# Two early mean subtractions moved behind later gates in the finish of a four-layer triangle-update kernel

## The reference

```
for each layer:
    xn    = layernorm(groupnorm(x))
    left  = (xn @ Wl [+ bl]) * sigmoid(xn @ Wlg [+ blg])     # two layers with a mask
    right = (xn @ Wr [+ br]) * sigmoid(xn @ Wrg [+ brg])
    out   = contraction of left and right over one token index, per channel
    x     = x + gated, projected layernorm(out)
```

## Time and profile before

| | |
|---|---|
| median of 3 runs | 2207.23 us (2206.90 to 2209.74) |
| the profiled execution's own time | 2204.45 us |
| its span (first to last instruction) | 2202.4 us |
| mean granted TensorE clock | 0.965 of full speed |
| TensorE busy | 1970.2 us (89%) |
| VectorE busy | 1734.3 us (79%) |
| ScalarE busy | 1655.7 us (75%) |
| GpSimd busy | 624.5 us (28%) |

### The profile page before, as it was taken

How to read it: one execution, slowest core, us unless ns; L and a number is a source line. 1 busy time by engine, 2 the same in 40 slices (tenths; PEclk the granted TensorE clock), 3 DMA queues, 4 the chain that set the end, 5 groups by cost and what they waited for, 6 DMA issues and landing times. The chain is left out here.

```text
span 2202.4 us, 45933 instructions
## 1 busy us (share of the span) xinstructions
PE 1970.2 (89%) x13950; PEld 1401.2 (64%) x13956; DVE 1734.3 (79%) x2934; ACT 1655.7 (75%) x2442; POOL 624.5 (28%) x590
## 2 busy tenths in 40 slices
PE   5798979699898998989989899899998989899998
PEld 4433959455433988965633598886553369798665
DVE  6788989989588878878958897877775888687664
ACT  3588869679788857758978785766877887596676
POOL 0100818265200000026410280732871000000655
PEclk8999999999999999989999999999999999999999
DMA  9488938279698928259979973917997984663798
GB/s 397 164 266 285 290 77 229 92 286 384 231 279 264 309 77 296 87 214 396 416 224 279 273 191 129 286 45 262 406 391 221 281 303 157 223 200 125 285 358 303
DMA packets 429363, 549.48 MB, mean 249 GB/s; under 512 B 14640, under 2 KB 325936, under 8 KB 412848
## 3 DMA queue, kind: packets, MB, share of 16 engines
q1 hardware_dynamic: 427648, 538.38, 73.1%
q10 hardware_dynamic: 1584, 9.51, 1.1%
HBM read 371.67 MB, written 176.16 MB: 249 GB/s over the span
## 5 line engine op out<-in xcount | busy, mean ns | idle before, releaser
L799 PE MATMUL bank<-whigh,kept 128*128 128x128 f16 x4096 | 507.5, 227 | 60.0 <-DMA kept<-XH 23.6
L799 PEld LDWEIGHTS bank<-whigh,kept 128*128 128x128 f16 x4096 | 466.9, 125 | 67.4 <-issue 53.9
L799 PE MATMUL bank<-wlow,kept 128*128 128x128 f16 x4096 | 506.5, 227 | 0.0
L799 PEld LDWEIGHTS bank<-wlow,kept 128*128 128x128 f16 x4096 | 467.5, 125 | 0.0
L1558 POOL TENSOR_TENSOR LR<-LR 128x512 f32<-128x512 f32 x128 | 186.6, 1477 | 526.6 <-DVE LR L1604 509.6
L821 ACT ACTIVATE sigs<-bank,small 128x256 f32<-128x256 f32 x512 | 237.2, 476 | 60.3 <-PE bank L799 53.6
L1549 POOL TENSOR_TENSOR LR<-LR,sum 128x2048 f32<-128x2048 f32 x30 | 136.6, 4552 | 510.2 <-DVE LR L1366 510.2
L663 PE MATMUL bank<-LR,cen 128*128 128x512 f32 x512 | 254.4, 622 | 21.3 <-DMA LR<-XT 9.5
L821 ACT ACTIVATE squares<-bank,small 128x256 f32<-128x256 f32 x512 | 236.2, 476 | 13.8 <-PE bank L799 6.6
L670 PE MATMUL bank<-LR,kst 128*128 128x512 f32 x512 | 240.9, 593 | 5.2 <-ACT LR L691 5.2
L836 POOL TENSOR_TENSOR msgs<-sigs,mask_sb 128x256 f32<-128x256 f32 x192 | 126.1, 672 | 378.6 <-ACT sigs L821 373.6
(11 more groups left out here) (174 smaller groups left out, 3616.4 us busy)
## 6 DMA issues: line engine op xcount, KB each, us to landing
kept<-XH SPq DMA_DIRECT2D x128, 512.0 KB, 6.0
LR<-XT SPq DMA_DIRECT2D x64, 1024.0 KB, 9.5
kept<-XHA SPq DMA_DIRECT2D x128, 512.0 KB, 4.6
LR<-XT SPq DMA_DIRECT2D x112, 512.0 KB, 5.4
XT<-LR SPq DMA_DIRECT2D x56, 1024.0 KB, 8.5
LR<-XH SPq DMA_DIRECT2D x64, 512.0 KB, 6.6
LR<-XHA SPq DMA_DIRECT2D x64, 512.0 KB, 5.7
OS<-kept SPq DMA_DIRECT2D x12, 2048.0 KB, 7.6
```

The lines of the kernel that those rows point to most:

```text
L799: last = pe.matmul(bank(g)[:, j * P:(j + 1) * P], tokens, w[:, half * P:(half + 1) * P], start=part == 0, stop=part == 1)
```

## The change

The subtraction of chunk 2 moves from step 7 to step 9 (`GL + 2`), that of chunk 3 from step 11 to step 12 (`GL + 5`), in the layers with the gate first. All other chunks stay.

```diff
             def _(dve):
                 def normalize(t):
-                    c = (t + AHEAD) // 4
-                    if (t + AHEAD) % 4 or not 0 < c < NCH:
+                    later = {2: GL + 2, 3: GL + 5} if gate_first else {}
+                    c = next((c for c, at_tile in later.items() if at_tile == t), (t + AHEAD) // 4)
+                    if later.get(c, 4 * c - AHEAD) != t or not 0 < c < NCH:
                         return
                     if c >= len(nrm):
                         dve.wait_ge(turned.s, turned.n + 4 * (c - len(nrm)) + 4)
```

## The result

| | before | after |
|---|---|---|
| median of 16 runs each | 2205.53 us (2201.33 to 2211.28) | 2210.7 us (2207.14 to 2216.01) |
| ratio of the times, 95% interval | | 1.0025 [1.0016, 1.0033] |
| the profiled execution's own time, and its span | 2204.45, 2202.4 us | 2209.22, 2207.3 us |
| mean granted TensorE clock | 0.965 | 0.958 |

The account below looks back on a forecast made before the run. TensorE was taken to set the pace in a finish's second half, its front pauses hanging on VectorE and GpSimd. +1.21 + 0 + 0 = +1.2 us took 2207.23 to 2208.4 us, range 2205.3 to 2211.3.

Parts of the forecast that it names:

- price of one fall: One tile behind the pause at half clock, 4.27 us for 1.94, 2.3 us lost: 2210.7 us in all, chance 0.07.
- The wait at s(2): VectorE's 2.83 us stand before chunk 2's subtractions, s(2), first finish: becomes other work, while the subtraction starts 1.65 us later.
- a(0): VectorE's residual add of tile 0, behind which chunk 2's subtractions were to stand in the first finish.
- p(1): TensorE's output product of tile 1: its pause, 1.05 us in the first finish and 0.60 in the second, was to go.
- The link of 7.10: From one chunk's subtractions to the next over GpSimd's multiply, 7.10 us: chunk 3's come +1.65 us, chunk 4's +1.21, first finish.
- p(17): TensorE's output product of tile 17, after a 2.07 us pause in the first finish: forecast 1.21 us later, at 486.07.
- The second finish: Finish of the second layer: depends on when TensorE's clock rises, taken as 0, with -0.7 to +1.0 us kept.
- Behind the third place: After chunk 6's subtractions wait 2.50 us for GpSimd's multiply of chunk 5: TensorE has no idle time to absorb anything.
- The chain's sum: Both finishes together: +1.21 for the first, 0 for the second, 0 for the moments' length, +1.2 us.
- The moments' own length: GpSimd's second-half moments, between its multiplies of chunks 4 and 5: taken as 0, with -0.5 us kept for each finish.
- The clock falls at the third place: Rival: pause before tile 17's output product grows to about 2.6 us; one fall 2210.7 us (0.07), two 2214.0 (0.04).
- a 0.50 clock behind p(17): Sign that the forecast is wrong: granted TensorE clock at 0.50 after tile 17's output product.

Follow-up runs that it names:

- before_fill: The kernel before, with tile 20's three out-gate matmuls issued four times over in both gate-first finishes: median 2209.01 us, ratio 1.0014.
- before_shift: The kernel before, with nine small extra matmuls behind each of the two gate-first finishes: median 2208.55 us, ratio 1.0021.
- before_again: The kernel before, unchanged, timed once more as a program of its own: median 2207.83 us, ratio 1.0002.
- after_again: The changed kernel, unaltered, timed a second time as a program of its own: median 2211.42 us, ratio to the kernel before 1.0016.
- after_shift: The changed kernel, with nine small extra matmuls behind each of the two gate-first finishes: median 2209.62 us, ratio to the kernel before 1.003.
- before_long: The kernel before, with one more small GpSimd operation behind the moments in the first two finishes, VectorE's order kept: median 2210.22 us, ratio 1.0015.
- after_fill: The changed kernel, with tile 20's three out-gate matmuls issued four times over in both gate-first finishes: median 2209.09 us, ratio to the kernel before 1.0021.
- after_dvem: The changed kernel, with the second half's moments taken from GpSimd to VectorE in the gate-first finishes: median 2205.29 us, ratio to the kernel before 1.0003.
- c3_only: The kernel before, with only chunk 3's subtraction moved and chunk 2's left in place: median 2211.46 us, ratio 1.0034.
- c2_only: The kernel before, with only chunk 2's subtraction moved and chunk 3's left in place: median 2205.95 us, ratio 1.0006.
- before_dvem: The kernel before, with the second half's moments taken from GpSimd to VectorE in the gate-first finishes: median 2210.48 us, ratio 1.0033.
- after_fill_again: The changed kernel with tile 20's out-gate matmuls issued four times over, timed a second time: median 2207.42 us, ratio to the kernel before 1.0007.

## Why the prediction was right in sign and wrong in size

The median after, 2210.7 us, lies within the forecast's range, but not by its mechanism. The range was counted from the median of three runs, 2207.23; the 16 runs have 2205.53. As a shift it reached up to +4.1 us, and the medians lie 5.2 apart. That 2210.7 is also the forecast's price of one fall is chance: there were two, and for two it gave 2214.0.

**The wait at s(2)** became work, as said: s(2) behind a(0), p(1) without a pause before it in the first finish. **The link of 7.10** held: s(3) at 456.67 and s(4) at 463.76, both released by GpSimd, where 456.65 and 463.75 were forecast. That they agree to 0.02 us is luck. The finish itself had begun 0.74 late in this execution, so the shifts by its own clock are +0.93 and +0.48, and s(2)'s is +0.94: p(0) came 0.7 sooner behind s(1) than in the execution of before. That p(17) is then +1.06 late, near the forecast's +1.21, takes a second error, the moments' length below. And p(0)'s place is no constant. In the five first finishes that have the changed order and the moments on GpSimd p(17) lay 1.03 to 2.61 us behind its place before, 1.96 in the mean. The three late ones are those in which the clock rises late, and s(2), now behind p(0), goes with it (7.93 or 7.91 behind s(1) in two, 9.35 to 9.47 in three). The old order has 43.94 or 43.95 in all four (before, before_fill, before_shift, before_again), though in before_again the clock stands at 0.50 until 447 us, 5 us behind s(1). Two stretches of after_again, where s(2) came at 9.47:

```profile
445.00:446.00 1.00, 1.00 (x6) 0.89 (x5) 0.03 (x1) 0.69 (x1) 1.00 (x1) 0.50 0.30 123
446.00:447.00 1.00, 1.00 (x5) 0.43 (x3) 0.67 (x1) 0.75 (x1) 1.00 (x1) 0.62 0.00 0
```

Here the granted clock rises late in 446 to 447 us, 6 us behind s(1) (440.36). In the execution of after it stood at 0.56 over 444 to 445 us and at 1.00 from there, so rose 3 us behind s(1) (441.65). The forecast weighed this dependence for the second finish and missed it for the first. **The second finish** was taken at 0 with -0.7 to +1.0. p(17) lies 0.84 earlier in the profiled execution, and 1.15 in the means of five against four. The lower end was the nearer one: the clock is back between 10 and 11 us behind s(1) (973.78), where before it took 15 (970.25 and the earlier trace rows):

```profile
983.00:984.00 1.00, 1.00 (x3) 0.48 (x2) 0.73 (x2) 0.69 (x1) 0.79 (x1) 0.50 0.02 8
984.00:985.00 1.00, 1.00 (x7) 0.60 (x6) 0.35 (x1) 0.00 (x0) 1.00 (x1) 0.91 0.00 0
```

**Behind the third place** TensorE does have pauses, of 1.11 and 0.40 us (before L1467 at 499.22 and 503.70; after, at 503.97 and 508.44), which the forecast took for none. They stayed as long and absorbed nothing.

**The chain's sum** is thus +1.96 - 1.15 = +0.8 us where +1.2 was forecast. **The moments' own length** was kept at 0 with up to -0.5 a finish, because of the rows in which only tensor_scalar operations were slow. They took 7.54 us (470.71 to 478.25) instead of 6.95. L1306, a tensor_tensor, went from 0.73 to 1.72. In the kernel before it started 0.16 ahead of s(5) (470.18 and 470.34), kept its 0.73, and s(5)'s first half took 1.65; after, it started 0.09 behind s(5) (471.30, 1.22 long), and was the one to be slowed. The moments began only 0.59 ahead of s(5), where they had been 0.8 ahead (0.26 was worked out). So that bound had the wrong sign, +0.59, and the second finish has it too (19.11 us from s(4) to s(6) instead of 18.55). The Trainium skill (GPSIMD Engine Reference, § 8 Key points) names VectorE's instruction as what contends and sets no condition on the kind that GpSimd runs; this trace agrees, where my reading of the rows did not.

**The step that failed** is the choice against a rival, the third: "The clock falls at the third place". The prediction worked out the pause ("to about 2.6 us"; 2.46 measured) and the price ("2.3 us lost"), and then left the clock up, with a chance of 0.04 for two falls, because it had stayed up over 2.07 us. Its own sign of being wrong, a 0.50 clock behind p(17), came in both finishes. The price is what eight tiles take over 16.97 us: 2.94, 2.93, 1.67, 1.67, 1.68 and 2.93 in the six finishes of three profiled executions (after, after_again, after_shift), 2.3 in the mean. Two falls are 4.6, and with the chain's 0.8 that is 5.4 us, against 5.3 ± 1.1 measured. With the scatter outside the finishes (below), so close an agreement is in part luck.

**What is shown:** the pause and the fall go together when the order is kept (before_long). The fall goes away when the pause is filled or removed, with the changed order in place (after_fill, after_dvem), and the finishes get their time back. In whole times it rests on before_long (+4.2 ± 2.2), c3_only against c2_only (+5.7 ± 2.8) and after_dvem against the changed kernel (-5.8 ± 1.6), less firmly on the fill. **What was only counted:** the fall came behind 9 of 10 pauses of 2.44 to 2.46 us and behind 1 of 8 of 2.06 to 2.09 us. The pause of 2.46 before p(5) in c2_only brought none. So a pause's length doesn't settle it alone. The Trainium skill (TensorE: Matmul & The Clock Gate, What's actually happening) says that the hardware's watching does not start with a kernel's work, but runs freely, so that one kernel's transitions differ from run to run. The unequal outcomes behind equal pauses, and prices from 1.5 to 2.9 us, fit that; no run here tests it. **What stays open:** before_fill and before_shift have a few matmuls more, finishes only about 0.5 us longer, and yet lie 2.6 ± 1.5 us above the kernel before (its 112 runs without before_again), where before_again lies at +0.6 ± 2.0. after_fill and before_dvem have a surplus of about 3 us outside their finishes too (after_fill_again only 1). The rest of the program took between 1918.6 and 1927.5 us in the profiled executions. Whether added instructions cost this elsewhere, or the intervals have missed, was not separated.

## What to carry to other kernels

A wait that is turned into work wins nothing if the next engine's chain behind it has no slack: write out the link (here 7.10 us from subtraction to subtraction) before counting the win. Where a shift makes TensorE stand a little longer at a place where it is otherwise dense, price the clock's fall there at full weight, at both levels, even if the clock stayed up over a slightly shorter pause: 0.4 us more standing brought falls in 9 of 10 finishes, which cost 1.5 to 2.9 us each. Before work is placed behind a matmul, look whether that matmul runs while the clock is still rising, since its time then differs from execution to execution.

## What the runs showed of the hardware

- Pauses of about 2.07 and 2.46 us before the same matmuls behaved differently: the clock fell 1 time in 8 and 9 times in 10, and a fall cost 1.5 (before_long, first finish) to 2.9 us (the changed kernel). Before p(5) in c2_only a pause of 2.46 brought no fall.
- A VectorE tensor_tensor of 128x256, 0.42 us in the kernel before, took 3.15 beside GpSimd's multiply of 128x2048 and ended when that was about done (444.98 + 3.15 = 448.13, against 443.32 + 4.52 = 447.84).
- GpSimd's small tensor_tensor slows like its tensor_scalar beside VectorE's subtraction: 0.73 to 1.72 us (L1306, before and after) and 1.70 us where its like takes 0.85 (L1308 and L1316). In the rows of L1306 and s(5) the operation that started later was the slowed one: s(5)'s half 1.65 instead of 1.22 when it came 0.16 behind, L1306 1.72 instead of 0.73 when it came 0.09 behind.
